# Loads of the weights of experts 2 to 5 issued behind the read of the list instead of ahead of the last sequence's row writes

## The reference, cut to what matters

```
x = x + attn_ref(layernorm(x), ...)            # 4 sequences: SSD mixer, then a gated MLP
x = x + ffn_ref(layernorm(x), gate_w, w1, w2, w3)

# inside ffn_ref, x_flat is [2048, 256], E = 8, TOP_K = 2, M = 896
router_probs = softmax(x_flat @ gate_w)
topk_w, topk_idx = top_k(router_probs, 2);  topk_w = topk_w / sum(topk_w)
h   = silu(x_e @ w1[e]) * (x_e @ w3[e])        # for the tokens of expert e
out = sum over the two experts of topk_w * (h @ w2[e])
```

## Time and profile before

| | |
|---|---|
| median of three runs | 813.77 us (813.22 to 813.79) |
| the profiled execution | 808.96 us |
| its span | 807.1 us |
| TensorE busy | 728.0 us, 90% |
| VectorE busy | 577.3 us, 72% |
| ScalarE busy | 227.4 us, 28% |
| GpSimd busy | 307.4 us, 38% |
| DMA | 43.74 MB, 54 GB/s over the span |

### The profile page before, as it was taken

The page is one execution under the profiler, slowest core; times in us unless marked ns, Lnnn a source line. Parts: engine busy times, 40 slices in busy tenths (PEclk is TensorE's granted clock), DMA queues, the critical chain, the costliest instruction groups (busy, mean ns, idle before and its releaser), DMA issues.

```text
span 807.1 us, 10348 instructions
## 1 busy us (share of the span) xinstructions
PE 728.0 (90%) x2751; PEld 464.5 (58%) x2752; DVE 577.3 (72%) x1370; ACT 227.4 (28%) x482; POOL 307.4 (38%) x505
## 2 busy tenths in 40 slices
PE   5888999899998999979608999999999999999992
PEld 3466547664667547655504666666666666666661
DVE  4686827868477865853634888888888888888870
ACT  1654544544444534631102111111111111111110
POOL 1266203740456315532242333344433344333422
PEclk9999999999999999999758999999999999999997
DMA  9800001000010000038617211111211112111111
GB/s 324 293 2 1 1 0 53 2 0 0 2 52 0 0 0 27 26 120 274 181 31 276 47 32 26 27 26 29 35 28 26 26 26 32 32 26 26 26 15 19
DMA packets 30167, 43.74 MB, mean 54 GB/s; under 512 B 4099, under 2 KB 23875, under 8 KB 30128
## 3 DMA queue, kind: packets, MB, share of 16 engines
q1 hardware_dynamic: 21600, 33.15, 12.3%
q0 software_dynamic: 8544, 10.30, 8.0%
HBM read 33.84 MB, written 9.75 MB: 54 GB/s over the span
## 4 chain that ended last, share of the span: by engine, by line
PE 64%; DVE 11%; issue 9%; POOL 9%; DMA 3%; ACT 2%; DVEq 0%; POOLq 0%; ACTq 0%; SPq 0%
PE ps L701 28%; PE ps L714 14%; PE ps L391 5%; PE ps L402 3%; PE ps L547 3%; PE ps L358 3%; PE ps L552 3%; POOL lists L1426 2%; POOL big L1404 2%; DVE big L1318 2%; PE ps L476 1%; DVE big L1026 1%; PE ps L566 1%; PE ps L434 1%; PE ps L374 1%
## 5 line engine op out<-in xcount | busy, mean ns | idle before, releaser
L1318 DVE STREAM_TRANSPOSE big<-big 32x224 f32<-32x224 f32 x608 | 244.8, 403 | 9.1
L701 PE MATMUL ps<-big 128*128 x624 | 242.7, 542 | 1.1 <-ACT big L932 1.1
L701 PEld LDWEIGHTS ps<-big 128*128 128x128 f32 x624 | 119.0, 191 | 106.1 <-issue 104.1
L1361 POOL TENSOR_TENSOR big<-big 128x1 f32<-128x1 f32 x179 | 56.6, 316 | 280.3 <-DVE big L1326 159.5
L714 PE MATMUL ps<-big 128*128 x546 | 124.5, 380 | 2.1 <-DVE big L1338 1.3
L714 PEld LDWEIGHTS ps<-big 128*128 128x128 f32 x546 | 100.8, 190 | 15.0 <-issue 2.9
L938 ACT ACTIVATE big<-ps 128x896 f32<-128x896 f32 x39 | 35.8, 917 | 217.2 <-PE ps L701 217.2
L358 PE MATMUL ps<-big 128*128 128x128 f32 (+1 forms) x327 | 52.3, 281 | 39.9 <-DMA big<-lists,big 16.0
L358 PEld LDWEIGHTS ps<-big 128*128 128x128 f32 (+1 forms) x327 | 39.8, 144 | 69.6 <-issue 28.6
L1333 DVE TENSOR_TENSOR big<-big,ps 128x896 f32<-128x896 f32 x39 | 42.4, 1087 | 47.5 <-PE ps L701 47.4
L1503 POOL DMA_INDIRECT out_rows<-big x39 | 63.3, 1623 | 23.8 <-issue 23.8
(11 more groups left out here) (173 smaller groups left out, 924.4 us busy)
## 6 DMA issues: line engine op xcount, KB each, us to landing
big<-in_w SPq DMA_DIRECT2D x24, 896.0 KB, 11.8
out_rows<-big SPq DMA_DIRECT2D x4, 512.0 KB
xn_rows<-big SPq DMA_DIRECT2D x4, 512.0 KB
big<-in_hidden SPq DMA_DIRECT2D x1, 1536.0 KB, 11.8
big<-in_in_proj SPq DMA_DIRECT2D x1, 1288.0 KB, 6.9
big<-in_gate SPq DMA_DIRECT2D x1, 640.0 KB, 12.8
big<-in_up SPq DMA_DIRECT2D x1, 640.0 KB, 8.7
big<-in_down SPq DMA_DIRECT2D x1, 640.0 KB, 9.2
```

What stands on the lines that cost most here:

```text
L701: last = mm(bank(bk + n)[:, 0:HALF], xT[:, k, :], expert_cols(e, off + k * M + n * HALF, HALF), start=(k == 0), stop=(k == KD - 1))
L1318: last = V.transpose(hTs[c * SQ:(c + 1) * SQ, half, :].rearrange("p (j t) -> p j t", j=MB)[:, :, q * SQ:(q + 1) * SQ], ha[q * SQ:(q + 1) * ...
L1361: G.tensor_tensor(idle[:, k:k + 1], half[:, 0:1], half[:, 0:1], ALU.add)
```

## The change

The two lines that load experts 2 to 5 move from ahead of SyncE's `body` for the last sequence to behind its read of the first list tile.

```diff
             sp.wait_ge(o_taken, SEQS * CH)
             sp.wait_ge(ssy_ready, SEQS * CH)
-            for e in range(EARLY, SOON):
-                load_next(e)
             body(SEQS - 1, True, False)
...
             sp.wait_ge(rec_out, 16 * CH * TOP * SEQS)
             sp.dma_start(rec0, lists[0:P, :]).then_inc(rec0_in, 16)
 
+            for e in range(EARLY, SOON):
+                load_next(e)
             for half in range(2):
                 sp.wait_ge(xg_in[half], 16)
             for e in range(SOON, E):
```

## The result

Timed on one chip with the kernel before, 20 runs of each, the changed kernel takes 817.37 us and the kernel before 814.35. The ratio is 1.0032, with a 95% interval of 1.0019 to 1.0045: 1.5 to 3.7 us more. (The median of before stood at 813.77 while it rested on three runs.) The profiled execution took 813.76 us with a span of 811.5; before it was 808.96 and 807.1.

A forecast was written before the change was run, and what follows sets the result against it. Bound: TensorE's work, plus exposed hand-over latency between token mixing and expert tiles. Terms: -0.4 (scatters) + 2.2 (gather 0) + 0 (others) = +1.8 us on the median 813.77, so 815.6 us; range 812.2 to 819.0.

The forecast's parts named there:

- gather 0: First gather of token rows before the expert tiles, on the critical chain: delayed by expert 2's load, +2.2 us.
- Rival A: No visible loss: the first gather gets through during the load's start-up, or scatters give back as much; 813.8 us, chance 0.17.
- between the two cases: Earlier gathers beside loads took 5.4 us (issued at 426.1) and 4.5 (at 441.8); delay 1.7 to 2.6, middle 2.2.
- The other bound that the text allowed for: SyncE's list read, just ahead of the load on its queue, held up as much: upper bound 5.2 us.
- The packet rule: DMA engines alternate queues packet by packet, so the first gather loses at most 1.8 us, making the sum +1.4.
- The list scatters: GpSimd's last list writes before the hand-over, no longer queued behind weights: -0.4 us, bounds 0 to 4.2 gain.
- Rival B: Faster: without weights the list scatters land as a gather does, wait falling from 7.00 below 4.8; 811.8 us, chance 0.13.
- The list gather: Gather of list entries at the hand-over: up to 2.6 us late, but covered by the first row gather, cost 0.
- The loads: Weights of experts 2 to 7 against their tiles: 10.1 us each, slack 15.5 to 11.2 us, cost 0.
- Rival C: Slower: adds of rows slow the loads, which come late for tiles 4 to 7; 820.0 to 835.6 us, chance 0.06.
- Rival D: Slower: adds of rows beside the loads become the bound for VectorE's weighing; 817.5 to 819 us, chance 0.09.
- The clock: TensorE's clock rise during the first L701 group: 7.88 us again, cost 0; at best 1.9 back, at worst 4.1 more.

The follow-up runs named there:

- e1: Changed kernel, but SyncE waits for the first gather's landing between the list read and loading expert 2; ratio to the kernel before 0.9985.
- e2: Kernel before, experts 2 to 5 still loaded early, but expert 6's load goes right behind the list read without waiting for the first two gathers; ratio 1.0042.
- e1b: The kernel of e1 run once more for its time; ratio to the kernel before 0.9990.
- e5: Changed kernel with only the last of the last sequence's eight list scatters issued; one run, read only for that scatter's landing, 4.65 us.
- e8: Changed kernel, but only w1 of expert 2 goes out behind the list read, all other loads wait for the first gather; ratio to the kernel before 1.0008.
- e6: Changed kernel, but expert 2's load also waits until TensorE has turned tile 1's rows; ratio to the kernel before 1.0091.
- b0: Kernel before, unchanged, profiled again in one run; its last list scatter landed after 9.78 us.
- e9: Changed kernel, but experts 2 and 3 load early as before, and 4 and 5 only behind the first gather; ratio to the kernel before 0.9996.

## Why the prediction was right, step by step

**The direction and the place.** The loss is where the sum put it, on gather 0, and the time lies inside the range. e1 takes it away and e2 puts it into the kernel before. Rival A, a gather that gets through in the load's start-up, is refuted by the 6.26. But the direction had a chance of 0.48 only, and the range reached from 812.2 to 819.0, so that the time fell inside it owes something to its width. Of its own signs of being right the prediction missed two, a first gather of 4.5 to 5.4 us (6.26) and a first L701 group near 427.7 (430.61).

**Gather 0, the term that was too small.** The sum had +2.2 and the runs showed +3.5 (6.26, 6.25, 6.50 and 6.21 against 2.8). The step that was mis-sized is the placing of gather 0 "between the two cases" in cost because it lay between them in time. Neither of the two gathers in the earlier trace rows bounds it. The one at 441.8 was issued 5.5 us behind its load, so only what was left of the load could hold it up, and it landed together with the load's end (441.8 + 4.5 = 446.3). The one at 426.1 was issued 0.14 us ahead of its load. Gather 0, 2.3 us behind its load, cost more than either. Other gathers of the same 128 rows say the same: in e1b one issued at 443.36, 1.25 us behind its load, took 6.8; in the changed kernel one issued at 446.39, 5.15 us behind, took 4.8, and one at 439.33, 8.34 us behind, took 2.9. In these runs the dearest place is soon behind the start of a load, and not the mean of what its two ends cost. The place alone doesn't give the price, though: in e5 a gather issued at 444.30, 4.78 us behind its load, took 6.6, and why is not shown. The other bound that the text allowed for, a list read held up by the load, did not come: 1.79 against 1.69. With 3.5 in place of 2.2 the sum would have been +3.1; the medians lie 3.0 apart.

**The packet rule.** The Trainium skill ("DMA: Bandwidth & Descriptors", section "Queues, rings and completion order") has each DMA engine take its queues in turn, packet by packet; the prediction drew from it +1.8 at the most. The runs showed 3.5. Whether the engines take the two queues in turn is not shown by these runs; as the prediction used it, the rule is no bound for a small transfer. In 425.3 to 427 the gather, issued by 424.01, had waited for more than a microsecond already, and not one of its packets was served, while 195 of the weights' were.

**The list scatters, -0.4.** Measured +0.22 in the first pair, about -1 in the later profiles. The term is small either way. Rival B, which had the wait fall below 4.8, is refuted for whole lists: with no weight load beside the scatters it stayed at 7.2 to 8.8. Its page rule, a fixed part of about 2 us (same page, section "Anatomy of one DMA"), does not agree with these scatters: even alone one takes 4.65. What stands beyond that is the queue of the scatters ahead (7.00 - 4.65 = 2.35 in the first profile), and not weights.

**The list gather, cost 0.** It landed 3.0 later than before (5.3 against 2.3) and cost nothing, as said. Its cover was thinner than the text made it: e8 shows it 3 us late with gather 0 nearly on time, and then it decides.

**The loads, cost 0.** Right. The forecast had 10.1 us for a load and expert 7 at 480.1; the loads came 9.51 to 10.31 apart and none was waited for. Rival C asked for loads over 12.0 us; e6 shows what it would have been like.

**Rival D, the adds.** Timelines after of GpSimd (first two rows) and VectorE (third):

```profile
455.55 1.65 POOL L1503 DMA_INDIRECT out_rows<-big  x1 [0.63 <-issue]
...
460.88 0.19 POOL L1361 TENSOR_TENSOR big<-big 128x1 f32<-128x1 f32 x1 [1.88 <-DMA out_rows<-big]
```

```profile
463.45 0.48 DVE L1326 TENSOR_SCALAR big<-ps,big 128x256 f32<-128x256 f32 x1
```

The add takes 460.88 - 455.55 = 5.3 us where it took 3.9: 1.4 more, and VectorE needs it 2.6 us later. The next two, issued at 464.87 and 474.13, took 5.6 and 5.8 and were in 2 us or more before the weighing that needs them. Hidden, as the forecast had it.

**The clock.** The first L701 group took 7.70 against 7.88, so 0 was right for this pair. It is not a constant: 9.08 in b0, 9.11 in e1b and 7.91 in e9, with the granted clock at 0.50 for a longer or shorter part of the tile: in b0 it stood at 0.50 until 440, 4.3 us into the tile, and in the changed kernel it was at 1.00 from 434, 3.4 us into it. Up to 1.4 us of difference between two profiles can come from here.

## What to carry to other kernels

A bulk load has its price at the moment when a small transfer on the critical path wants its turn, and one load is enough. Let the queue that issues bulk loads wait until the first dependent gathers have landed. In e1 that wait cost nothing, because load 2 had still landed 11 us ahead of its tile (440.11 against 451.08). When the price of running beside a load is read from a trace, look at where in the load the small transfer was issued, and take one that was issued as far behind the start as yours will be; here those issued in the load's second half were mostly too cheap. And when the critical gather is mended, look at the other small transfers of the same hand-over, which had been hidden behind it.

## What the runs showed of the hardware

- A gather of 128 rows of 1 KB that is issued 2.2 to 2.3 us behind a whole load, which reaches about 400 GB/s, lands after 6.1 to 6.5 us in place of 2.8. With rows of 896 B in place of 3584 B a gather issued in the middle of a load still takes 6.4.
- A list scatter of 128 entries of 8 B takes 4.65 us to land when it stands alone, and the last of eight that are issued in two groups of four, 1.27 us apart, takes 7.0 to 9.8. In the last 5 us before that landing the DMA engines show a share of 0.00. So an empty DMA share does not say that nothing is under way; what holds the entries up in that time is not shown.
- The same kernel showed 7.00, 9.78 and 9.03 us for that landing in three profiles, and its fastest and slowest of the first 20 runs lie 5.5 us apart (811.54 to 817.08). The 95% interval of the ratio of 20 runs each is 0.26% wide, so a difference of 0.1% between two kernels cannot be seen through this.
